# Marking nodes on VectorE alone, and four TensorE signals a batch, in a graph layer's edge loop

## The reference, cut to what matters

```python
def ssp(x):
    return jax.nn.softplus(x) - LOG2
h = x @ W_in2f
Wij = ssp(rbf @ Wf1 + bf1) @ Wf2 + bf2      # two filter layers, 64 -> 256 -> 256, for every edge
Wij = Wij * dist_cut
x_ij = h[idx_j] * Wij                       # the message of an edge
m = jax.ops.segment_sum(x_ij, idx_i, num_segments=n_atoms)
m = ssp(m @ Wo1 + bo1) @ Wo2 + bo2
return x + m
```

## Time and profile before

| | us |
|---|---|
| median of 3 executions | 6996.84 (6991.12 to 7000.83) |
| the profiled execution, its own time | 6996.57 |
| its span, first to last instruction | 6995.0 |
| PE, DVE, ACT, POOL busy in the span | 5083.2, 4251.5, 2800.8, 3454.5 |
| mean granted TensorE clock | 0.895 |

### The profile page before, as it was taken

How to read it: one execution, slowest core, us unless ns; L and a number is a source line. 1 busy time by engine, 2 the same in 40 slices (tenths; PEclk the granted TensorE clock), 3 DMA queues, 4 the chain that set the end, 5 groups by cost and what they waited for, 6 DMA issues and landing times. The chain is left out here.

```text
span 6995.0 us, 120144 instructions
## 1 busy us (share of the span) xinstructions
PE 5083.2 (73%) x25530; PEld 3822.0 (55%) x25595; DVE 4251.5 (61%) x13005; ACT 2800.8 (40%) x7992; POOL 3454.5 (49%) x4373
## 2 busy tenths in 40 slices
PE   3222388888545657888888389978999997777776
PEld 2222166666344425666666366654657775666575
DVE  4223766666346757899999777764424335666622
ACT  0000166666331152666766311113533333666522
POOL 4666188888734620888888022212310002888621
PEclk9999699999767957999999699999998998888788
DMA  6411133333425741222223255554430002444453
GB/s 217 156 44 36 38 103 102 100 102 101 99 70 160 211 116 52 68 68 68 68 68 67 64 170 180 187 175 119 134 97 21 13 9 69 131 129 130 98 152 121
DMA packets 787072, 719.52 MB, mean 103 GB/s; under 512 B 349384, under 2 KB 692973, under 8 KB 786382
## 3 DMA queue, kind: packets, MB, share of 16 engines
q1 hardware_dynamic: 596344, 372.06, 19.0%
q0 software_dynamic: 120064, 280.26, 15.0%
q10 hardware_dynamic: 70486, 65.22, 2.7%
HBM read 520.74 MB, written 201.60 MB: 103 GB/s over the span
## 5 line engine op out<-in xcount | busy, mean ns | idle before, releaser
L1460 PE MATMUL l0e_ps_w<-l0e_wf,l0e_hidT 128*128 128x256 f32 x1760 | 450.4, 414 | 156.8 <-DVE l0e_shifted L1395 140.2
L1460 PEld LDWEIGHTS l0e_ps_w<-l0e_wf,l0e_hidT 128*128 128x128 f32 x1760 | 355.6, 207 | 297.2 <-issue 222.4
L1138 POOL DMA_INDIRECT l0e_rows<-table,l0e_idx x440 | 456.8, 1038 | 82.7 <-issue 70.1
L1128 POOL DMA_INDIRECT l1e_rows<-table,l1e_idx x440 | 431.3, 980 | 121.9 <-issue 121.9
L1138 POOL DMA_INDIRECT l3e_rows<-table,l3e_idx x440 | 442.8, 1006 | 89.7 <-issue 88.7
L3520 ACT ACTIVATE l1e_weighted<-l1e_rows,l1e_power 128x64 f32<-128x64 f32 x1760 | 463.1, 334 | 16.8 <-ACT l1e_power L3511 9.4
L818 PE MATMUL l0n_cell_ps<-l0n_cell_hot,l0n_cell_before 128*128 128x175 bf16 x390 | 133.5, 342 | 421.1 <-issue 233.6
L1157 POOL TENSOR_SCALAR l3e_onehot<-net_columns,l3e_rec 128x128 f32<-128x128 f32 x220 | 140.6, 639 | 602.5 <-DMA l3e_rec<-records_by_dst 595.0
L897 POOL DMA_INDIRECT records_by_src<-l0n_rec_src,l0n_pos_at_src x390 | 377.7, 968 | 119.0 <-issue 113.1
L3461 PE MATMUL l1e_ps_row<-net_ident,l1e_logit 128*128 128x128 f32 x1760 | 277.3, 280 | 132.5 <-DVE l1e_logit L3656 131.7
L726 DVE CUSTOM_DVE_ANT_0 l0n_cell_picked<-l0n_cell_hot,l0n_cell_ps 128x175 f32<-128x175 bf16 x390 | 114.7, 334 | 406.9 <-remote 317.3
(11 more groups left out here) (845 smaller groups left out, 15754.6 us busy)
## 6 DMA issues: line engine op xcount, KB each, us to landing
counts<-l1f_total ACTq DMA_DIRECT2D x272, 128.0 KB
l1fg_w_in<-in_L_ffn_W SPq DMA_DIRECT2D x32, 1024.0 KB
l1fg_w_out<-in_L_ffn_W SPq DMA_DIRECT2D x32, 1024.0 KB
records_by_dst<-l0n_blank_dst SPq DMA_DIRECT2D x5, 6512.0 KB
l3e_rec<-records_by_dst SPq DMA_DIRECT2D x110, 296.0 KB
l2d_counts<-counts SPq DMA_DIRECT2D x208, 128.0 KB, 2.5
l2d_counts<-counts POOLq DMA_DIRECT2D x192, 128.0 KB
l3fg_w_in<-in_L_ffn_w SPq DMA_DIRECT2D x16, 1024.0 KB
```

Of the source, the lines that this page charges most:

```text
L1128: pool.indirect_dma_start(at(self.rows[b], k, self.width), None, self.table, bass.IndirectOffsetOnAxis(self.idx[b][:, k:k + 1], 0)).then_i ...
L1138: pool.indirect_dma_start(at(self.rows[b], k, self.width), None, self.table, bass.IndirectOffsetOnAxis(self.idx[b][:, k:k + 1], 0)).then_i ...
L1460: ins = pe.matmul(ps_w[:, k, m * D:(m + 1) * D], hidT[b][:, c * WIDE + (2 * k + m) * P:c * WIDE + (2 * k + m + 1) * P], at(wf2, c, D), sta ...
```

## The change

POOL's two marking instructions are taken out, and with them their wait. DVE's marking instruction makes all four tiles, by the helper `mark_nodes`, and signals PE through `hot_ready`; `half_ready` is no longer used here. PE raises `hidden`, `filters` and `summed` once a batch, at the last matmul of the batch, and all that wait for them count in batches: 1 + 1 + 1 signals and the one of `turn`, where there were 2 + 2 + 2 and the one of `turn`. DVE no longer waits for `hot_ready` before it gives records back.

```diff
@@ gpsimd
-            def onehot_read(pool, q, i, b):
-                if not isinstance(i, int) or i:
-                    pool.wait_ge(summed, (q - RING) * TWO + TWO)
-
             on = lambda step: lambda q, i, b: step(pool, q, i, b)
-            skewed(pool, (1, on(g.gather_tile(0))), (0, on(g.hot_tile(0, onehot_read))), (1, on(g.gather_tile(1))), (0, on(g.cast)),
-                   (1, on(g.gather_tile(2))), (0, on(g.hot_tile(1))), (1, on(g.gather_tile(3))),
+            skewed(pool, (1, on(g.gather_tile(0))), (1, on(g.gather_tile(1))), (0, on(g.cast)),
+                   (1, on(g.gather_tile(2))), (1, on(g.gather_tile(3))),
@@ vector, message
-                    dve.wait_ge(filters, n + 1)
+                    dve.wait_ge(filters, q + 1)
...
-                dve.wait_ge(g.hot_ready, q + 1)
@@ vector, add
-                    dve.wait_ge(summed, n + 1)
+                    dve.wait_ge(summed, q + 1)
@@ vector, hot
-                    dve.wait_ge(summed, (q - RING) * TWO + TWO)
+                    dve.wait_ge(summed, q - RING + 1)
                 dve.wait_ge(g.rec_loaded[b], i * 16 + 16)
-                half = [P, BATCH // 2, P]
-                dve.tensor_tensor(tiled(g.onehot[b][:, :], P)[:, BATCH // 2:BATCH, :],
-                                  net.columns[:, :].unsqueeze(1).to_broadcast(half),
-                                  g.column(b, g.placed.near)[:, BATCH // 2:BATCH].unsqueeze(2).to_broadcast(half), ALU.is_equal)\
-                    .then_inc(g.half_ready, 1)
+                mark_nodes(dve, net, g.onehot[b], g.column(b, g.placed.near)).then_inc(g.hot_ready, 1)
@@ tensor, hide
-                    pe.matmul(ps_h[:, c, :], wf1[half, :], rbfT[b][half, :], start=True, stop=True).then_inc(hidden, 1)
+                    ins = pe.matmul(ps_h[:, c, :], wf1[half, :], rbfT[b][half, :], start=True, stop=True)
+                ins.then_inc(hidden, 1)
@@ tensor, filter
-                    ins.then_inc(filters, 1)
+                ins.then_inc(filters, 1)
@@ tensor, add
                 pe.wait_ge(g.hot_ready, q + 1)
-                pe.wait_ge(g.half_ready, q + 1)
...
-                    ins.then_inc(summed, 1)
+                ins.then_inc(summed, 1)
@@ scalar, power
-                    act.wait_ge(hidden, HC * q + c + 1)
+                    act.wait_ge(hidden, q + 1)
```

## The result

The changed kernel takes 7176.4 us (median of 4 runs, 7166.1 to 7187.5) beside 6994.6 us for the kernel before on the same chip: a ratio of 1.0258, 95% interval 1.0242 to 1.0273. It is 2.6% slower, where 1.9% faster was forecast. The profiled execution has a span of 7176.2 us. From the first matmul of the first filter layer to the last of the sums the loop now takes 1161 us instead of 984 us, and these 178 us are nearly all of the 181 us between the two spans.

The account below looks back on a forecast made before the run. POOL was taken to bound the edge loop at 8.92 us a batch; 1.21 us saved less 0.03 for the port, said as 1.20, times 110 batches gives 132 us: 6996.6 to 6865 us, range 6843 to 6895 (about 0.85).

Parts of the forecast that it names:

- The parts on POOL: Edge loop: losing two marking instructions saves 1.43 us a batch; with gather changes 1.31, less shifted waiting 1.21.
- DVE's marking: Edge loop: one DVE instruction marks four tiles in 687 ns instead of 428, 0.26 us more a batch, under POOL's need.
- port: Edge loop: a two-operand DVE instruction can hold up a POOL instruction starting under it; taken as 0.03 us a batch.
- The signals: Edge loop: PE's seven signals become four; first filter layer at most 0.57 us later, within 1.83 us slack; cost taken as nothing.
- The sign that I had set for them: Edge loop: DVE or PE waiting for a signal of PE instead of rows would show that the later signals bite.
- How fast would the others go with rows in hand?: Edge loop's lead-in, with POOL some batches ahead: PE's pace over six batches is 6.89 us a batch.
- the next floor: Edge loop: the limit below POOL's 8.92 us a batch, said to lie 2.03 us lower.
- The sum itself: Edge loop: 110 batches x 1.20 us = 132 us, taking 6996.6 us to 6865 us, 1.9% faster.
- Rival 1: Edge loop: another engine takes over; at 8.0 us a batch the gain is 101 us, time 6895; chance 0.10.
- Rival 2: Edge loop: DVE's longer marking holds up one POOL instruction 0.26 us every batch; gain 104 us, time 6892; chance 0.08.
- Rival 3: Edge loop: gathers can't follow faster because transfers set their pace; nothing gained, 6997; chance 0.03.
- Rival 4: Edge loop: half of PE's work at TensorE's lower clock, 10.3 us a batch; 155 us slower, 7152; chance 0.03.

Follow-up runs that it names:

- seven signals: Against the kernel before, the marking is moved to DVE but TensorE keeps its seven signals a batch: 7143.2 us, ratio 1.0211.
- 128x64 kernel: Changed kernel plus two spare 128x64 instructions a batch on POOL, in the old marking's places: 6937.3 us, 0.9944 of the kernel before.
- 128x128: Changed kernel plus two spare 128x128 instructions a batch on POOL, in the old marking's places: 6987.3 us, 1.0014 of the kernel before.

## Why the prediction was wrong

- **The parts on POOL were right.** The marking is gone, gathers stand 0.30 us apart (timeline), and they take 0.98 us. POOL's own need is (421.9 + 132.3 + 178.7 + 28.9 + 23.1 + 23.0 + 22.3 us and some 4 us of gaps) / 107.75 batches = 7.74 us; I had 8.92 - 1.20 = 7.72.
- **DVE's marking was right** (687 ns), and the **port** did no harm: the gathers' mean fell.
- **The signals cost next to nothing by themselves**, as I had it (ratio 1.0009). The sign that I had set for them, DVE or PE waiting for a signal of PE, did come, but it comes with seven signals as well (32 stalls). Where signals come late anyway, the merged ones cost 33 us more.
- **The step that failed is "How fast would the others go with rows in hand?"** I read 6.89 us from the lead-in the earlier trace rows and made it the next floor, as if the other engines' speed did not depend on what POOL does. But in the lead-in POOL still marked nodes between its gathers. That was the very condition that the change takes away: in the changed kernel's own lead-in a batch takes 11.55 us. With the rest at 8%, the signals of TensorE hold its consumers up to 11 us, the others need 10.43 us a batch, and POOL, the former bound, waits for them.
- **The sum itself holds as long as that condition does.** The 128x64 kernel shortens POOL's two instructions from 682 to 528 ns, so by my working POOL should gain 2 x 0.15 = 0.31 us a batch; it gained 8.91 - 8.53 = 0.38, and the kernel 6973.7 - 6937.3 = 36 us.
- **The rivals.** Rival 1 was right in that POOL no longer sets the pace, but it had a busy engine in its place, at 8.0 us; here no engine is near full. Rival 2 fell: the gathers' mean is 979 ns, where it was 1038. Rival 3 fell: gathers do follow at 1.27 to 1.30 us. Rival 4 named 7152 us, near the 7176 measured, but by luck. Its sign came, the granted clock fell from 0.95 to 0.86 while TensorE stood still more; but TensorE was busy 827.95 / 107.75 = 7.7 us a batch where it had been 794.33 / 107 = 7.4, so stretched work can be 0.3 us of the 1.5 us that a batch lost, and 7.7 is far from the 10.3 that rival needed. No rival had signals that come late.
- **What I overlooked** was on record in the trace: 291 us of "remote" waits behind finished matmuls, in a stage in which POOL issues transfers without a pause. I had read the loop that was changed, and no other place where its engines already did what the change would make them do.

What stays open is the mechanism: whether matmuls or only their signals are held, by what, and why a rest of POOL lets them go. Nor does a hold end only when POOL stops: in the loop, ACT was released 2.5 us after POOL's last gather began, but DVE (1302.21 us) before it, and in the preparing stage DVE was also released in the middle of a run (309.38 us).

## What to carry to other kernels

Before an engine is relieved of work, look in the same trace for a place where it already runs without that work, and see how its neighbours fare there. Where GpSimd issues indirect transfers in a stretch in which TensorE's results are waited for, compare the end of a matmul with the start of its consumer; a gap of several us with the label "remote", or with a transfer of an earlier stage as its releaser, was the sign here. A few short instructions among the transfers were then worth more than they cost; try their number and size, since with too many of them GpSimd was the bound again (8.99 us a batch with 128x128, 8.53 with 128x64).

## What the runs showed that I had not expected

- In the changed kernel the consumers of TensorE's results start up to 11.4 us after the matmul's recorded end, while GpSimd issues indirect transfers with 8% of rest; in the kernel before, in the same loop, at most 1.1 us. The increments of DVE and ACT in the same stretch are recorded within 0.01 us of the end of their instructions.
- A 128x1 instruction on GpSimd takes 0.35 us in the edge loop, a 128x64 one 0.53, a 128x128 one 0.70, all beside transfers; in the preparing stage the 128x1 one takes 0.31 to 0.41 us.
- Where GpSimd waited for its own two gathers, the wait took 2.75 us a batch, about twice the time expected from the landing of rows.
